# A transformer layer with routed experts on one core: the gate's bias moved to TensorE, the logits' copy to ScalarE, the one-hot differences to GpSimd

## What is computed

```python
h = einsum('bsk,kh->bsh', concat([pos_emb, nest_emb, seg_emb]), W)      # (16, 256, 128)
h = h + attention(layernorm(h))                # 8 heads of 64, in chunks of 128 tokens, without a softmax over tokens
xf = layernorm(h)
logits = xf @ Wg + bg                          # 8 experts
vals, idx = top_k(softmax(logits), 2); vals = vals / (sum(vals) + 0.01)
y[e] = relu(xf @ W1[e] + b1[e]) @ W2[e] + b2[e]
h = h + sum over the two chosen e of vals * y[e]
```

## Time and profile before

| | us |
|---|---|
| median of 3 runs (352.64 to 353.0) | 352.75 |
| the profiled execution, as timed | 354.0 |
| its span, first to last instruction | 352.2 |
| busy in it: TensorE / VectorE | 325.4 / 302.1 |
| busy in it: ScalarE / GpSimd | 255.4 / 197.3 |

### The profile page before, as it was taken

One profiled execution on the slowest core, in us unless ns is written; L12 is line 12 of the kernel. 1 busy time (PEld: TensorE's weight loads), 2 busy tenths in 40 slices (PEclk: granted clock), 3 DMA queues, 4 the chain that ended last, 5 costly groups with the idle time before them and its releaser, 6 DMA issues.

```text
span 352.2 us, 11441 instructions
## 1 busy us (share of the span) xinstructions
PE 325.4 (92%) x3017; PEld 289.2 (82%) x3017; DVE 302.1 (86%) x1190; ACT 255.4 (73%) x754; POOL 197.3 (56%) x346
## 2 busy tenths in 40 slices
PE   8947999999999999999978699999998999999983
PEld 3615888888878787878867698999998999999972
DVE  6686999999989999999996487999986877778986
ACT  1636889999979898999975477776766776776730
POOL 7011320777775677767747367788875454554520
PEclk9986999999999999999998899999999999999999
DMA  6066760000000100000012022323333222226857
GB/s 168 19 183 167 217 227 2 28 34 27 29 27 34 36 29 25 25 25 34 34 35 76 19 69 73 87 85 86 107 120 92 77 68 78 73 75 204 249 174 243
DMA packets 33130, 30.46 MB, mean 86 GB/s; under 512 B 4701, under 2 KB 27320, under 8 KB 33080
## 3 DMA queue, kind: packets, MB, share of 16 engines
q1 hardware_dynamic: 25848, 18.81, 18.5%
q0 software_dynamic: 4224, 9.18, 7.6%
q10 hardware_dynamic: 3008, 1.89, 1.8%
HBM read 16.42 MB, written 13.44 MB: 85 GB/s over the span
## 4 chain that ended last, share of the span: by engine, by line
PE 45%; DVE 29%; issue 13%; DMA 4%; ACT 3%; DVEq 2%; SPq 2%; ACTq 0%
PE ps_oy L1818 6%; PE ps_out L1808 6%; PE ps_v L1818 6%; PE ps_q L1808 5%; DVE qk_max L1087 3%; DVE k_prime L1093 3%; DVE q_prime L1093 3%; PE ps_oy L1729 3%; PE ps_out L1713 3%; DVE stats L1070 2%; PE ps_qT L1701 2%; PE ps_qT L1800 2%; PE ps_k L1808 2%; DVE h L1082 1%; DVE heads_out L1105 1%
## 5 line engine op out<-in xcount | busy, mean ns | idle before, releaser
L777 POOL DMA_INDIRECT y_dram<-heads_out,place x68 | 69.4, 1021 | 45.9 <-ACT heads_out L969 36.5
L755 POOL DMA_INDIRECT slots_dram<-rows,row_id x64 | 64.6, 1010 | 20.4 <-issue 19.9
L960 ACT ACTIVATE k_prime<-ps_out,b_T 128x128 f32<-128x128 f32 x105 | 31.4, 366 | 19.0 <-PE ps_out L1808 18.7
L960 ACT ACTIVATE k_prime<-ps_q,b_T 128x128 f32<-128x128 f32 x108 | 31.9, 365 | 17.0 <-PE ps_q L1808 16.8
L1818 PE MATMUL ps_oy<-w_tile,k_prime 128*128 128x128 f32 x288 | 38.4, 276 | 1.4 <-issue 1.3
L1713 PE MATMUL ps_out<-context,qT 128*128 128x130 f32 x256 | 37.7, 291 | 0.0
L1818 PE MATMUL ps_v<-w_tile,k_prime 128*128 128x128 f32 x280 | 37.1, 276 | 0.5 <-issue 0.4
L1808 PE MATMUL ps_out<-sT,w_tile 128*128 128x128 f32 x280 | 37.1, 275 | 0.0
L1818 PEld LDWEIGHTS ps_oy<-w_tile,k_prime 128*128 128x128 f32 x288 | 35.0, 192 | 2.1 <-issue 2.1
L1729 PE MATMUL ps_oy<-out_w,oT 128*128 128x128 f32 x256 | 36.4, 286 | 0.0
L729 POOL TENSOR_TENSOR rstd<-moments,ln_eps 128x4 f32<-128x4 f32 (+1 forms) x19 | 3.7, 195 | 57.2 <-DVE moments L1076 56.6
(11 more groups left out here) (282 smaller groups left out, 865.2 us busy)
## 6 DMA issues: line engine op xcount, KB each, us to landing
qkv_rows<-slots_dram SPq DMA_DIRECT2D x71, 72.0 KB
y_sum<-y_dram SPq DMA_DIRECT2D x14, 256.0 KB, 3.4
w_all<-in_L_ffn_W SPq DMA_DIRECT2D x1, 2048.0 KB, 14.0
w_all<-in_L_ffn_W SPq DMA_DIRECT2D x8, 256.0 KB, 4.3
out<-h SPq DMA_DIRECT2D x6, 256.0 KB, 3.5
y_dram<-heads_out,place POOLq DMA_INDIRECT x68
y_dram<-y_sum SPq DMA_DIRECT2D x2, 512.0 KB, 5.6
slots_dram<-rows,row_id POOLq DMA_INDIRECT x64, 2.3
```

The costliest lines, as they stand in the source:

```text
L755: nc.gpsimd.indirect_dma_start(slots_dram[:, :], bass.IndirectOffsetOnAxis(row_id[:, place_of(p, a), j, k:k + 1], 0), rows[:, place_of(p, ...
L777: nc.gpsimd.indirect_dma_start(y_dram[:, :], bass.IndirectOffsetOnAxis(place[:, a, :], 0), y[:, a, :], None).then_inc(s_placed[a], 16)
L960: last = nc.scalar.activation(hT[:, a % 2, c, :], ps_up[a % 2][0][:, c * P:c * P + P], ACT.Relu, bias=b1_T[:, bass.ds(experts[0] * FC + c, ...
```

## The change

The bias of the gate is loaded as one row instead of 128 equal ones. `gate_product` gets one more matmul ahead of its two: a row of 128 ones (`ones_row`, set once by GpSimd) times the bias row, repeated for the two tiles, opens the accumulation, and the two gate matmuls add to it. ScalarE gets `logits_copy(p - 2)` as the last thing in its sequence, which copies the 16 columns from PSUM; VectorE's `read_logits` leaves the sequences, and its wait for `s_lgr` in front of `residual` stays, now as a wait for ScalarE. For the last two sequences, in the experts' stage, VectorE still reads the logits, by a plain copy. `change_of` moves from VectorE to GpSimd: for p - 3 and p + 2 both within range it stands in `scatter` in place of the addition into `spare`, and for the first five sequences it stands alone ahead of `scale` (at p = 1 also ahead of `make_padding`). In VectorE's odd half `invert` moves ahead of `stats_of`.

```diff
             def scatter(p, a, first=0, last=2 * TOP, changed=None):
...
-                take_wait()
+                if changed is None:
+                    take_wait()
+                else:
+                    step.wait()
+                    change_of(changed, 1 - a)
...
+            def logits_copy(p):
+                act.wait_ge(s_lg, p + 1)
+                nc.scalar.activation(logits[:, :, :], ps_ln[:, 0:2 * E].rearrange("p (j e) -> p j e", j=2), ACT.Copy)\
+                    .then_inc(s_lgr, 1)
...
                 if live(t + 2, TILES):
                     k_exp(t + 2, 1 - a, 0)
                     qT_copy(t + 2, 0)
+                if live(p - 2):
+                    logits_copy(p - 2)
...
                 if live(p + 2):
                     dve.wait_ge(s_h, p + 3)
-                    change_of(p + 2, a)
-                    stats_of(p + 2, stats)
                 if live(p):
                     inverted = invert(t)
+                if live(p + 2):
+                    stats_of(p + 2, stats)
...
                 if live(p - 2):
-                    read_logits(p - 2)
                     dve.wait_ge(s_lgr, p - 1)
...
+                nc.tensor.matmul(ps_ln[:, 0:2 * E].rearrange("p (j e) -> p j e", j=2), ones_row[:, :],
+                                 gate_b[:, None, :].to_broadcast([1, 2, E]), start=True, stop=False, skip_group_check=True)
                 for j in range(2):
                     last = nc.tensor.matmul(ps_ln[:, j * E:j * E + E], x2T[:, a, j * P:j * P + P], gate_w[:, :],
-                                            start=True, stop=True)
+                                            start=False, stop=(j == 1), skip_group_check=True)
```

More of the change, by code:

```diff
@@ L255, in lm_tower_kernel @@
         gate_w = sb("gate_w", [P, E])
-        gate_b = sb("gate_b", [P, E])
+        gate_b = sb("gate_b", [1, E])
+        ones_row = sb("ones_row", [1, P])
         w1_all = sb("w1_all", [P, E * FF])
@@ L682, in _ @@
             nc.gpsimd.memset(ones[:, :], 1.0)
+            nc.gpsimd.memset(ones_row[:, :], 1.0)
             for r in range(RING):
@@ L745, in weigh, with change_of, scatter @@
                                         weight[:, :, None].to_broadcast([P, 2, E]), ALU.mult).then_inc(s_weighed, 1)
-            def scatter(p, a, first=0, last=2 * TOP):
+            def change_of(p, a):
+                pool.wait_ge(s_hot, p + 1)
+                wait(pool, s_v, 2 * p - 2)
+                nc.gpsimd.tensor_tensor(change[:, a, :], one_hot[:, a, P:P + S], one_hot[:, a, 0:S], ALU.subtract)\
+                    .then_inc(s_change, 1)
+            def scatter(p, a, first=0, last=2 * TOP, changed=None):
                 pool.wait_ge(s_id, p + 1)
@@ L762, in sequence @@
                     weigh(p - 3, 1 - a)
-                    scatter(p - 3, 1 - a)
+                    if live(p + 2):
+                        scatter(p - 3, 1 - a, changed=p + 2)
+                    else:
+                        scatter(p - 3, 1 - a)
+                elif live(p + 2):
+                    change_of(p + 2, a)
                 if isinstance(p, int) and p == 1:
@@ L766, in sequence @@
                 scale(p, a)
-            sequences(pool, step, sequence, 16)
+            sequences(pool, step, sequence, 14)
             def place_y(n, a, i, experts):
@@ L806, in _ @@
             act.dma_start(gate_w[:, :], w_gate[:, :]).then_inc(s_gate_w, 16)
-            act.dma_start(gate_b[:, :], b_gate.rearrange("(o d) -> o d", o=1).to_broadcast([P, E])).then_inc(s_gate_w, 16)
+            act.dma_start(gate_b[:, :], b_gate.rearrange("(o d) -> o d", o=1)).then_inc(s_gate_w, 16)
             def table_mid(n):
@@ L1059, in hot @@
                                         ALU.is_equal).then_inc(s_hot, 1)
[L1061 to L1066, removed]
             def stats_of(p, st):
@@ L1113, in residual, with read_last_logits @@
                 nc.vector.tensor_tensor(at, ps_oy[:, 0:D], at, ALU.add).then_inc(s_h2, 1)
-            def read_logits(p):
+            def read_last_logits(p):
                 dve.wait_ge(s_lg, p + 1)
-                nc.vector.tensor_tensor(logits[:, :, :], ps_ln[:, 0:2 * E].rearrange("p (j e) -> p j e", j=2),
-                                        gate_b[:, None, :].to_broadcast([P, 2, E]), ALU.add).then_inc(s_lgr, 1)
+                nc.vector.tensor_copy(logits[:, :, :], ps_ln[:, 0:2 * E].rearrange("p (j e) -> p j e", j=2)).then_inc(s_lgr, 1)
             def find_top():
@@ L1278, in gates @@
             def gates(p):
-                read_logits(p)
+                read_last_logits(p)
                 dve.wait_ge(s_lgr, p + 1)
```

## The result

The changed kernel takes 357.88 us (median of 4 runs, 357.68 to 358.88), the kernel before beside it 352.88 (352.64 to 353.02): a ratio of 1.0148, 95% interval 1.0133 to 1.0163. It is 5.0 us slower where the forecast had 0.9. The profiled execution was timed 357.98 and has a span of 356.2 us against 352.2. The profiled one of before was timed 354.0, 1.1 above its median, so that the two profiles show 4.0 of the 5.0 us.

The account below looks back on a forecast made before the run. VectorE was taken as the bound in most turns, with ScalarE and TensorE in turn setting a sequence's time after the change. The stretches summed to +0.9 us on the 352.75 us median, 353.65 us, range 351.3 to 355.3.

Parts of the forecast that it names:

- What bounds before: VectorE bounds most turns, busy 38.98 of 39.26 us ahead of the loop; TensorE bounds the position product's stretch.
- The ring: Closed chain through q_exp, TensorE's gate, ScalarE's logits copy and the next q_exp: 10.05 us a sequence, between 9.81 and 10.18.
- S: Mark in each sequence, 2.28 us before the gate product's start, from which a turn is summed to the next sequence's.
- b: Added bias matmul on TensorE ahead of the gate's two: taken as 0.22 us, bounds 0.03 and 0.26.
- c: ScalarE's logits copy ahead of the next q_exp: taken as 0.15 us, bounds 0.10 and 0.24.
- The program's turn: Loop turn, now behind the copy instead of in ScalarE's idle time: 0.1 us on each of three, +0.3 us.
- The start: Stretch up to the third sequence: VectorE's 0.21 us gained twice, -0.4 us (0 to -0.6).
- Sequences 14 and 15: Last sequences, VectorE-bound: some 0.4 us less, +0.25 at the last gate product, together -0.1 us.
- experts' stage: Two gate products with an added bias matmul each, one counted: +0.2 us (0 to 0.5).
- GpSimd still waits for the moments: Denies the rival that GpSimd becomes the bound, its change taking over 1.1 us: 355.5, up to 357 us; chance 0.08.
- the one-hots on VectorE: Rival: GpSimd's change holds a VectorE one-hot each sequence, making VectorE's turn 10.1 us: 354.1 us; chance 0.06.
- Rival 1: VectorE stays the bound because the logits copy is in time: -5.5 us, 347.2 us; chance 0.12.

Follow-up runs that it names:

- e3: The full change without the bias matmul, the gate's bias left out of the logits: 0.9932 of the kernel before, period 9.74 us.
- e4: The full change with ScalarE's logits copy moved from the end of its sequence to the head of the next: 1.0149 of the kernel before.
- e1: The kernel before with only the one-hot differences moved to GpSimd, VectorE still adding the bias and reading the logits: 0.9935 of the kernel before.
- e2: The kernel before with only the gate part, bias on TensorE and logits copied by ScalarE, differences still on VectorE: 1.0154 of the kernel before.
- e8: The full change with the logits copied by VectorE instead of ScalarE, bias matmul kept: 1.0111 of the kernel before.
- e5: The full change with ScalarE's logits copy placed behind the first q_exp of the next sequence: 1.0160 of the kernel before.
- e17: The kernel before with only the differences on GpSimd, run once more on another run's chip: 0.9948 of the kernel before.
- e12: The full change with the one-row f32 bias matmul moved ahead of the embedding product, logits in other columns of the bank: 1.0030 of the kernel before.
- e13: The full change with the bias as three bf16 rows, its matmul ahead of the embedding product: 0.9968 of the kernel before.
- e16: The full change with the bf16 bias ahead of the embedding product and the logits copy behind the next first q_exp: 1.0020 of the kernel before.

## Why the prediction was wrong, by its steps

- *What bounds before*: the text reads VectorE as the bound from its busy share, but the same row has TensorE busy 39.01 us beside VectorE's 38.98, of 39.26: busy time does not tell the two apart. What does is who waits, ScalarE for q_prime, and this reading held.
- *The ring* was forecast rightly: its members, 6.84 us from first q_exp to S (6.85), S to S as ScalarE and TensorE in turn, VectorE waiting at the residual. Without b it is 9.74 us (e3) as against 9.68 + c.
- *The bias matmul, b* is the step that failed: "I take 0.22, near the upper one, since it is f32 like the gate's and TensorE loads 128 columns of weights for it, whatever the number of rows". The load's length does not hang on the rows, but its overlap with its neighbours does: 0.51 us with one row, twice the upper bound. With 96 or 128 rows it is 0.21. Both bounds came from matmuls of 128 rows. The sequences of the trace have no matmul of few rows between others (one of 32 rows stands behind the last gate, at 192.07), and the two loads around the context product, which show the lost overlap, were not read; the sentence of the Trainium skill on the drain (TensorEngine Tiling (Array Packing), Key Properties), which spoke against this change, was not weighed. In the eleven turns from sequence 0 to 11 that is 11 x (0.51 - 0.22) = 3.2 us.
- *The copy, c*: 0.09 us, under its lower bound of 0.10; in eleven turns 0.06 each the other way, -0.7.
- *The program's turn*: 0.1 us was put on each of three; two cost 0.45 and 0.42 (10.73 and 10.70 us against 10.28), and the entry into the loop 0.17 (10.45): 1.0 instead of 0.3, +0.7. It had been hidden in ScalarE's idle time; behind the copy nothing hides it, as e4 shows.
- *The start*: -0.4 was expected; the +0.67 lies within a scatter that no edit here explains. e1, with the differences off VectorE, has its first gate at 57.81, no earlier than before.
- *Sequences 14 and 15* (the table's 11 to 13): -1.0 instead of -0.1. The last gap is 10.83 us instead of 12.23. It is as short in e2 and in e8 (11.05), long in e1 (12.21) and in e5 (12.49). e17, the same kernel as e1, has 11.08: the gap differs by 1.1 us between two executions of one kernel, so that it is no measure of an edit. Why is left open.

Together 3.2 - 0.7 + 0.7 + 1.1 (start) - 0.9 - 0.4 (experts' stage) = 3.0 more than the +0.9 forecast, 3.9 us, against a span that grew by 4.0. The start and the last sequences, both within the scatter of the runs, nearly cancel, and so do the copy and the program's turn; what is left is b.

The rivals: VectorE did not stay the bound, GpSimd still waits for the moments, and the one-hots on VectorE take 0.30 to 0.31 us, so none of the three came. What the text did not see at all is the second ring, through TensorE's order and `context_copy`. It was there to be read: S to the end of the context product in the profile of before is 129.57 + 0.69 - 126.85 = 3.41 us (its row is shown above), and from the context copy to the next S it is 6.85 less one q_exp, 6.2: some 9.6 us. Rival 1's 347.2 us was out of reach for this change even with b at nothing: e3 has VectorE free of both pieces of work and no bias matmul, and its period is 9.74 us, its time 0.9932 of the kernel before. GpSimd's 0.66 us lie between the estimate from rows, 0.54, and the 0.75 that was worked out from the GPSIMD Engine Reference of the Trainium skill.

## What to carry to other kernels

A chain of engines that work in order is closed by everything that stands between two waits in each queue, not only by the instruction that reads the result: before work moves to an engine that "has time", sum each ring through that engine, and ask what the ring with the next instruction in the queue would be. Size an added matmul from a row with the same number of rows, and give a one-row term as many rows as its neighbours have (here 96 or more), or put it where the engine waits anyway. Of a change with two halves, time each alone: one half was worth 0.5 to 0.65% and the other cost 1.5%, and would have brought nothing even with its bias for free.

## What the runs showed of the hardware

- An f32 matmul of 1, 32 or 64 rows between f32 matmuls of 128 costs the path 0.30 us more than one of 96 or 128 rows (0.51 against 0.21 us a sequence), though its weight load is as long (0.29 and 0.30).
- Where a matmul starts an accumulation in a PSUM bank, another one that is open in other columns of the bank does not go on: its next product does not add to what stood there (e12, e13). The output's distance from the full one is 0.1103 of its norm; computing the layer without the bias in these twelve sequences gives 0.1102, and without it in all sixteen 0.1271, as e3 has. PSUM — Partial Sum Buffer of the Trainium skill (The four PSUM rules) says this of the whole bank, and e16, where the second product does not start anew, keeps its bias.
- ScalarE's turn of the program loop costs some 0.4 us between the copy and the q_exp (0.56 us, against 0.17 in e4, where it lies ahead of the copy's wait).
- GpSimd's subtraction of two 96 x 256 bf16 tiles takes 0.66 us (once 1.04), VectorE's costs its queue 0.21.
